# Attention and experts on one core: head outputs and score maxima re-laid by DMA, both score matmuls ahead of the maxima, the ends of six groups moved into the last two head pairs, and a ninth pair's maxima moved into the expert phase

## The reference

```python
x = L0_attn_z                                   # 4 batches x 1024 tokens x 128 features, float32
xn = _layernorm(x, axis=-1)
s = _L0_attn_ref(xn, ...)    # layernorm again, 16 heads of 8, softmax(q k^T / sqrt(8)) v, projection, + residual
g = _silu(_L0_ffn_ref(xn, ...))   # 8 experts 128 -> 512 -> 128 with exact gelu, top-2 softmax weights
x = x + s * g
```

## Time and profile before

| | before |
|---|---|
| median of 3 runs | 1122.94 us (1122.94 to 1123.12) |
| profiled execution: time, span | 1122.82 us, 1121.0 us |
| PE, DVE, ACT, POOL busy | 94%, 80%, 78%, 32% of the span |
| granted TensorE clock | 0.992 of full speed |

### The profile page before, as it was taken

The page is one execution under the profiler, slowest core; times in us unless marked ns, Lnnn a source line. Parts: engine busy times, 40 slices in busy tenths (PEclk is TensorE's granted clock), DMA queues, the critical chain, the costliest instruction groups (busy, mean ns, idle before and its releaser), DMA issues.

```text
span 1121.0 us, 17375 instructions
## 1 busy us (share of the span) xinstructions
PE 1054.6 (94%) x6009; PEld 449.6 (40%) x6041; DVE 893.9 (80%) x1647; ACT 870.7 (78%) x1189; POOL 361.1 (32%) x551
## 2 busy tenths in 40 slices
PE   4998999999999999999999999999999999999995
PEld 3666666666666666662212122212221221212123
DVE  5747778777878787657999999999999999999615
ACT  6876667676767676667888888888889888888981
POOL 4785657566666666452100010000000000000001
PEclk9999999999999999999999999999999999999999
DMA  5332221323141413223111111111111111111102
GB/s 180 119 106 59 82 72 50 95 50 104 31 119 37 113 35 93 50 68 106 45 45 30 45 44 46 31 44 34 55 40 35 44 44 45 30 44 30 31 1 76
DMA packets 84993, 67.42 MB, mean 60 GB/s; under 512 B 9277, under 2 KB 71402, under 8 KB 84906
## 3 DMA queue, kind: packets, MB, share of 16 engines
q1 hardware_dynamic: 84906, 66.32, 21.5%
HBM read 51.08 MB, written 15.20 MB: 59 GB/s over the span
## 4 chain that ended last, share of the span: by engine, by line
PE 31%; ACT 19%; DVE 3%; issue 2%; POOL 0%; ACTq 0%; DVEq 0%; POOLq 0%
ACT p_ring L798 18%; PE psum L987 13%; PE psum L965 10%; PE psum L928 4%; PE psum L1000 2%; DVE neg_max_half L1243 1%; PE psum L1021 1%; ACT o_sb L789 1%; DVE x_out L1315 0%; DVE msa_t L1296 0%; PE psum L939 0%; DVE y L1302 0%; PE psum L1013 0%; DVE y L1308 0%; ACT neg_max_t L774 0%
## 5 line engine op out<-in xcount | busy, mean ns | idle before, releaser
L798 ACT ACTIVATE p_ring<-psum 128x1024 f32<-128x1024 f32 x512 | 500.8, 1023 | 65.3 <-PE psum L965 61.6
L1243 DVE TENSOR_REDUCE neg_max_half<-psum 128x1 f32<-128x512 f32 x768 | 486.6, 685 | 37.3 <-PE psum L928 28.2
L965 PE MATMUL psum<-q_stack,k_stack 51*128 51x512 bf16 x1024 | 278.4, 382 | 13.3 <-ACT p_ring L798 4.1
L987 PE MATMUL psum<-p_ring,v_sb 128*9 128x512 f32 x2048 | 268.2, 596 | 0.4 <-ACT o_sb L789 0.4
L928 PE MATMUL psum<-k_max_stack,q_max_stack 48*128 48x512 bf16 x768 | 249.9, 384 | 5.8 <-DVE neg_max_half L1243 5.5
L761 ACT ACTIVATE h_hi<-psum,cols 128x512 fp32r<-128x512 f32 x192 | 132.5, 690 | 134.1 <-PE psum L878 133.2
L1261 DVE TENSOR_REDUCE neg_max_half<-psum 128x1 f32<-128x512 f32 x256 | 169.5, 684 | 55.1 <-PE psum L914 48.7
L634 POOL TENSOR_TENSOR h_lo<-h_split,h_hi 128x512 fp32r<-128x512 f32 x128 | 164.8, 1292 | 134.0 <-ACT h_split L764 133.8
L965 PEld LDWEIGHTS psum<-q_stack,k_stack 51*128 51x128 bf16 x1024 | 60.1, 94 | 305.8 <-ACT p_ring L798 281.8
L584 POOL CAST neg_max_parts<-neg_max_rest 128x16 bf16<-128x16 f32 x32 | 6.3, 198 | 509.6 <-DVE neg_max_rest L1252 509.5
L876 PE MATMUL psum<-xn_t_hi,w_hi 128*128 128x512 f32 x256 | 144.6, 565 | 0.7 <-DVE neg_max_half L1261 0.5
(11 more groups left out here) (123 smaller groups left out, 1023.8 us busy)
## 6 DMA issues: line engine op xcount, KB each, us to landing
expert_w_bc<-expert_w_dram SPq DMA_DIRECT2D x64, 256.0 KB, 4.9
k_rows_dram<-qk_parts SPq DMA_DIRECT2D x24, 256.0 KB, 3.1
q_max_stack<-q_rows_dram SPq DMA_DIRECT2D x64, 96.0 KB, 2.5
k_max_stack<-k_rows_dram SPq DMA_DIRECT2D x64, 96.0 KB, 2.5
q_stack<-q_rows_dram SPq DMA_DIRECT2D x64, 96.0 KB, 2.5
k_stack<-k_rows_dram SPq DMA_DIRECT2D x64, 96.0 KB, 2.5
q_rows_dram<-qk_parts SPq DMA_DIRECT2D x8, 384.0 KB, 2.6
xz<-in_L_attn_z_dram SPq DMA_DIRECT2D x8, 256.0 KB, 3.5
```

The source lines that it names most:

```text
L798: act.activation(p_sb[:, n % PR, a, :, :].rearrange("p h t -> p (h t)"), scores_bank[s % 2], ACT.Exp, scale=SCALE).then_inc(S("P"), 1)
L965: i = pe.matmul(scores_bank[s % 2][:, hh * TG:(hh + 1) * TG], k_s[rows, slot, kt * P:(kt + 1) * P], q_s[rows, slot, a * TG:(a + 1) * TG], ...
L987: i = pe.matmul(o_bank[at:at + VR, :], v_sb[:, b * KT + kt, 2 * (p % PB) + hh, :], p_sb[:, n % PR, a, hh, :], start=(kt == 0), stop=(kt == ...
L1243: dve.tensor_reduce(mx[:, p % MXR, c, hh * NT + t:hh * NT + t + 1], ring_bank(("max", u)), AX.X, ALU.max, negate=True).then_inc(S("R"), 1)
```

## The change

- **Maxima.** `m_t` and `neg_max_t` are gone. `sp_store_max` now stores `nmp` straight from its 128 partitions, transposing by its access pattern: 128 x 48 bf16 elements, each its own run of 2 bytes in DRAM. `neg_parts(p)` waits for the store of pair p-2.
- **Heads' outputs.** `o_t` and `head_out` are gone for pairs 0 to 30. At block 2 of the next pair `sp_heads` sends the output rows of `o_sb` to their place in `heads` (4 DMAs of 8 rows of 2 KB) and the sums to `den` spread over 128 partitions (4 DMAs of 32 runs of 64 bytes); at block 5 DVE takes reciprocals of [128 x 16] (`head_rden`), SP stores them to DRAM (block 6) and loads them back broadcast to 8 partitions each (block 7, 4 DMAs). POOL multiplies whole groups (`normalise_heads`). `o_copy` now waits for those DMAs of two pairs before. Only the last pair is turned on PE (`last_out`, `last_turn`) and projected separately (`project_last`).
- **Scores first.** Inside `scores` both score matmuls come first and signal ACT, and then come the tiles of maxima; the first half of a block takes 2 of them, the second the rest.
- **Ends.** `project`, `sum_y`, `gate_y`, `y_turn` and `finish` of groups 0 to 5 run from block 243 on, one group in two blocks. The gate is formed in the expert phase with tanh for groups 0 to 6 (silu(x) = 0.5 x (1 + tanh(x/2)), the 0.5 in `finish`), and for group 7 as before at the end. All gating products are on DVE.
- **Nine pairs.** EARLY_PAIRS is 9; the early tiles come every 3/4 slot instead of every 27/32, and end at the same slot. 736 tiles are left for the 240 blocks.

```diff
-        EARLY_PAIRS = 8
+        EARLY_PAIRS = 9
...
-        EARLY_AT = [HT + 4 + (27 * m) // 32 for m in range(EARLY)]
+        EARLY_AT = [HT + 4 + (3 * m) // 4 for m in range(EARLY)]
...
+            upto = [min(len(SINGLES), -(-((n + a) * len(SINGLES)) // MAX_BLOCKS)) for a in range(2)]
+            return (upto[0], min(upto[0] + 2, upto[1]), upto[1])[half]
...
-        TAIL = BLOCKS - KT + O_TURN + 1
+        ENDS_FROM = BLOCKS - 2 * KT + 3
...
         def sp_store_max(sp, p):
-            sp.wait_ge(S("mTc"), p + 1)
-            sp.dma_start(m_dram[p], nmT[:, p % 2, :]).then_inc(S(f"m_st{p % 2}"), 16)
+            sp.wait_ge(S("nmp"), p + 1)
+            sp.dma_start(m_dram[p].rearrange("m c -> c m"), nmp[:, p % 2, :, :, :].rearrange("p h i t -> p (h i t)"),
+                         allow_slow_non_contiguous=True).then_inc(S(f"m_st{p % 2}"), 16)
...
+        def sp_heads(sp, p):
+            b, slot = p // PB, p % 2
+            sp.wait_ge(S("oe"), p + 1)
+            for hh in range(2):
+                h = 2 * (p % PB) + hh
+                for a in range(2):
+                    at = VC * (2 * hh + a)
+                    sp.dma_start(heads[DH * h:DH * (h + 1), 2 * b + a, :], o_sb[at:at + DH, slot, :])\
+                        .then_inc(S(f"o_st{slot}"), 16)
+            n = TG // den.shape[2]
+            for t in range(4):
+                sp.dma_start(den[t * n:(t + 1) * n, slot, :],
+                             o_sb[VC * t + DH:VC * t + VR, slot, :].rearrange("a (n k) -> a n k", n=n))\
+                    .then_inc(S(f"den{slot}"), 16)
...
+                if p > 0 and kt == 2:
+                    sp_heads(sp, p - 1)
+                if p > 0 and kt == 6:
+                    sp_rden_out(sp, p - 1)
+                if p > 0 and kt == 7:
+                    sp_rden_in(sp, p - 1)
...
         def neg_parts(p):
                 if p > 1:
-                    pool.wait_ge(S("mT"), p - 1)
+                    pool.wait_ge(S(f"m_st{p % 2}"), 16 * (p // 2))
...
+            def normalise_heads(b):
...
+                for a in range(2):
+                    g = 2 * b + a
+                    pool.tensor_tensor(heads[rows, g, :], heads[rows, g, :], rden_t[rows, b % 2, a, :], ALU.mult)\
+                        .then_inc(S("hn"), 1)
...
+                if p in (18, 25, PAIRS - 1):
+                    normalise_heads((18, 25, PAIRS - 1).index(p))
+            normalise_heads(B - 1)
...
+                def gate():
+                    wait(act, "acc", g, E - 1, E - 1)
+                    act.wait_ge(S("qp"), 2 * (g + 2))
+                    act.activation(gt, ffn[:, g, :], ACT.Tanh, scale=0.5).then_inc(S("gate"), 1)
...
             def o_copy(p):
                 if p > 1:
-                    act.wait_ge(S("ot"), p - 1)
+                    act.wait_ge(S(f"o_st{p % 2}"), 64 * (p // 2))
+                    act.wait_ge(S(f"den{p % 2}"), 64 * (p // 2))
...
-                for k, hh in enumerate((first, 1 - first)):
+                for hh in range(2):
                     rows = slice(HALF * hh, HALF * hh + SROWS)
                     i = pe.matmul(scores_bank[s % 2][:, hh * TG:(hh + 1) * TG], k_s[rows, slot, kt * P:(kt + 1) * P],
                                   q_s[rows, slot, a * TG:(a + 1) * TG], start=True, stop=True)
-                    if k:
-                        i.then_inc(S("S"), 1)
-                    for u in units[k::2]:
-                        max_scores(u)
+                i.then_inc(S("S"), 1)
+                for _, u in singles:
+                    max_scores(u)
...
+            def project_last(g):
+                pe.wait_ge(S("tmc_a" if g == BESIDE else "tmc"), 1)
+                pe.matmul(project_bank(g)[:, :], wp_last[:, :], msaT[:, g - BESIDE, :], start=False, stop=True)\
                     .then_inc(S("tp"), 1)
...
+                ends.setdefault(4 * g, []).append(lambda g=g: project(g))
+                ends.setdefault(4 * g + 2, []).append(lambda g=g: y_turn(g))
...
+                def gated():
+                    wait(dve, "gate", g, 1, 1)
+                    dve.scalar_tensor_tensor(ffn[:, g, :], gt, 1.0, ffn[:, g, :], ALU.add, ALU.mult)\
+                        .then_inc(S("gated"), 1)
...
+            def head_rden(p):
+                slot = p % 2
+                dve.wait_ge(S(f"den{slot}"), 64 * (p // 2 + 1))
+                if p > 1:
+                    dve.wait_ge(S(f"r_st{slot}"), 16 * (p // 2))
+                dve.reciprocal(rden[:, slot, :], den[:, slot, :]).then_inc(S("rd"), 1)
...
+                if p > 0 and kt == 5:
+                    head_rden(p - 1)
```

More of the change, by code:

```diff
@@ L766, in gelu @@
                     return step
[L767 to L774, removed]
+                def gate():
+                    wait(act, "acc", g, E - 1, E - 1)
+                    act.wait_ge(S("qp"), 2 * (g + 2))
+                    act.activation(gt, ffn[:, g, :], ACT.Tanh, scale=0.5).then_inc(S("gate"), 1)
+                plan = {i: [gelu(i)] for i in range(HT)}
+                if g < NG - 1:
+                    plan[4 * E + 6] = [gate]
+                return plan
             def hi(ns):
@@ L779, in _ @@
             prepare_first(pre, experts, {9: hi(range(2)), 12: hi(range(2, 4)), 18: hi(range(4, RAW))})
[L780 to L781 removed]
+            expert_phase(experts, pre, first={2 * (n - RAW) + 5: hi([n]) for n in range(RAW, 2 * E)})
             def o_copy(p):
@@ L804, in _ @@
             o_copy(PAIRS - 1)
-            for g in range(NG):
-                act.activation(ffn[:, g, :], ffn[:, g, :], ACT.Silu).then_inc(S("gate"), 1)
+            act.activation(ffn[:, NG - 1, :], ffn[:, NG - 1, :], ACT.Silu).then_inc(S("silu"), 1)
+            act.wait_ge(S("tm"), 1)
+            act.activation(msaT[:, 0, :], bank[0][0:2 * DH, :], ACT.Copy).then_inc(S("tmc_a"), 1)
         @block.tensor
@@ L990, in pv, with last_out, last_turn @@
                 i.then_inc(S("PV"), 1)
[L992 to L998, removed]
+            def last_out():
+                pe.wait_ge(S("oe"), PAIRS)
                 for j in range(TT):
-                    i = pe.transpose(to[:, j * P:(j + 1) * P], o_sb[:, p % 2, j * P:(j + 1) * P], ident[:, :])
+                    i = pe.transpose(o_bank[:, j * P:(j + 1) * P], o_sb[:, (PAIRS - 1) % 2, j * P:(j + 1) * P],
+                                     ident[:, :])
                 i.then_inc(S("ot"), 1)
[L1004 to L1013, removed]
+            def last_turn(a):
+                pe.wait_ge(S("od"), 1)
+                pe.wait_ge(S("P"), 2 * BLOCKS)
+                for j in range(TT):
+                    m = pe.transpose(bank[a][0:2 * DH, j * P:(j + 1) * P], msa[:, a, j, :], ident[:, :])
                 m.then_inc(S("tm"), 1)
@@ L1046, in _ @@
                 p, kt = divmod(n, KT)
-                halves, turns = block_items(n)
-                at = 2 * (n - TAIL)
+                halves = block_items(n)
+                at = 2 * (n - ENDS_FROM)
                 scores(2 * n, halves[0])
-                for kind, k in turns:
-                    m_t(k) if kind == "mT" else o_t(k)
                 for step in ends.get(at, []):
@@ L1062, in _ @@
             pv(BLOCKS - 1)
-            for at in range(2 * (BLOCKS - TAIL), 2 * BESIDE + 2):
+            for at in range(2 * (BLOCKS - ENDS_FROM), 4 * BESIDE + 1):
                 for step in ends.get(at, []):
                     step()
-            o_t(PAIRS - 1)
-            for step in (msa_turn, project, y_turn):
-                for g in range(0 if step is y_turn else BESIDE, NG):
+            last_out()
+            for g in range(BESIDE, NG):
+                project(g)
+            for a in range(2):
+                last_turn(a)
+            for step in (project_last, y_turn):
+                for g in range(BESIDE, NG):
                     step(g)
```

196 lines of the change are left out of this document (91 added, 105 removed).

## The result

| | before | after |
|---|---|---|
| median | 1122.94 us (4 runs) | 1580.35 us (4 runs, 1569.96 to 1580.8) |
| ratio to before | | 1.407, 95% interval 1.4005 to 1.4128 |
| span of the profiled run | 1121.0 us | 1568.2 us |
| first exp, last copy of outputs | 510.3, 1092.3 us | 586.3, 1555.3 us |
| granted TensorE clock | 0.992 | 0.84 |

The forecast was 1089 us, 1066 to 1124. The kernel is 41% slower, on the side of the first rival (chance 0.15, priced at 1151 for a store of 15 us).

What follows compares the result with a forecast made beforehand. PE was taken to bound the expert phase, and late second scores with closely coupled PE, ACT and DVE the attention. 1121.0 - 42 + 9 + 5 - 16 + 10 = 1087.0 us of span, plus 1.8: 1089 us, range 1066 to 1124.

Steps and rivals of the forecast that it cites:

- first rival: At head_rden, block 5: the store of 2-byte runs holds up DVE and the kernel gets slower, 1151 us; chance 0.15.
- part 5: SP's DMAs: an 8 us store of maxima delays the sums only if issued shortly before them, +10 us.
- 1, 30 pairs with maxima: Attention: with both scores first, a pair takes 16.8 us; -42 us, bounds -63 and -15.
- 2, expert phase: Expert phase: 32 more tiles on PE and more DVE work; +9 us, bounds +6 and +15.
- 3, ends beside the last two pairs: Last two pairs: the ends of six groups make PE late; +5 us, bounds +2 and +9.
- 4, tail: After the last output copy: 12.7 us in place of 28.7; -16 us, bounds -17 and -13.
- my formula: At block 5: lateness of the sums from a store issued at t, taking S; +10 us in total at 8 us.

Runs made afterwards that it cites:

- flat_store: The changed kernel with its store of the maxima not transposed, 128 runs of 96 bytes in place of 6144 of 2, maxima scrambled: 1080.5 us, ratio 0.9625.
- pe_turn_mixed: The changed kernel with maxima turned on TensorE and stored as before, score matmuls again alternating with tiles of maxima: 1110.5 us, ratio 0.9898.
- dve_eight: dve_turn with eight pairs' maxima in the expert phase in place of nine: 1086.0 us, ratio 0.967.
- four_byte: The changed kernel with the store in 3072 runs of 4 bytes in place of 6144 of 2, maxima scrambled: 1310.4 us, ratio 1.1675.
- late_in: The changed kernel with the reciprocals read back one pair later in SyncE's order: 1478.4 us, ratio 1.317.
- pool_queue: The changed kernel with the stores of pairs 9 to 31 issued from GpSimd's queue: 1444.0 us, ratio 1.2865.
- dve_turn: The changed kernel with maxima transposed on VectorE in 32x32 blocks and stored as 128 runs of 128 bytes: 1083.0 us, ratio 0.965.

## Why the prediction was wrong

One step failed, part 5, the DMAs: in its price (8 us for a store that took 25.1 to land) and in its reach (a wait added only for stores shortly before the sums, where each store cost about 7 us in the expert phase and 18 in the attention). The other parts stand, read in flat_store, whose store takes 2 us.

| step | forecast | measured in flat_store against before |
|---|---|---|
| 1, 30 pairs with maxima | -42 | -42.9 (first exp to last reduction: 503.6 for 546.5) |
| 2, expert phase | +9 | +12.2 (first exp at 522.5 for 510.3) |
| 3, ends beside the last two pairs | +5 | +4.1 (last reduction to last copy: 39.6 for 35.5) |
| 4, tail | -16 | -16.2 (12.5 for 28.7) |
| 5, stalls on the store | +10 | 0 here; +490 of span in the changed kernel |

In all 1121.0 - 42.9 + 12.2 + 4.1 - 16.2 = 1078.2, the span of flat_store.

**Part 1** was right with its mechanism. In flat_store, windows and waits of mid-attention, against the earlier trace rows:

```profile
840.00:980.00 140.00, 137.94 (x1024) 28.86 (x1024) 131.39 (x222) 133.12 (x144) 7.44 (x26) 1.00 0.21 54
```

```profile
ACT p_ring L853 <- PE psum L999: 16.7, 39, 1.6
```

and ACT's timeline, where the exps stood four in a row before:

```profile
784.86 11.99 ACT L853 ACTIVATE p_ring<-psum 128x1024 f32<-128x1024 f32 x12 [0.23 <-PE psum L999]
```

ACT is busy 133 of 140 us where it was 125, and from 560 to 1010 us waits 39 times for scores, 16.7 us in all, where it was 103 times and 52.8 us (over 490 us). `pe_turn_mixed` shows the order's share in this, 13 us. In `dve_eight` 32 more tiles cost 18.3 us, 0.57 each: the tile isn't hidden behind TensorE and ScalarE, and its price is near VectorE's pitch of 0.634.

**Part 2** was mis-sized. The bound of +6 to +15 held in flat_store and in dve_eight (13.3), but 32 tiles cost about 0.4 us each and not 0.25. The price of a tile was misread: the prediction divided 82.8 us by 256 tiles, but the row of 82.8 us holds 224 matmuls, so a tile is 0.37 us (in flat_store 92.0 us for 256, 0.36). With 32 x 0.37 = 11.8 in place of 8 its own sum gives about +13. The waits for VectorE grew too, to 17.1 us in flat_store from 10.4; what they add was not tried.

**Part 5**, as the prediction put it: "nearest are the small ones and I take 21 ns: 8 us." A packet of 2 bytes took 46 ns on average and a store 25.1 us to land. My bounds of 3.8 to 30 us held it, but my value came from packets 128 times larger, as if size alone mattered, and the chance of the rival was set by nearness to those. The model itself was wrong too: it took a store to be over when its packets are. In four_byte they are started within 5.5 us and the landing takes some 15.

The Trainium skill ("VectorE: DVE Perf Modes", The three transpose paths) gave the right warning, but the estimate by its factor, 9.3 us, is too small against the 25.1 us measured. (At 9.3 us my formula adds 6 us, not the 5 that the prediction says.)

The reach failed more. "It delays the sums only if it is issued shortly before them" leaves out two things that the runs show. With S = 25 the lateness t + S + 3 - 11.5, summed over all 22 stores of the attention but pair 31's, is about 270 us and would put the kernel at 1349. It took 1580. The expert phase gives 64 of the 490 us of span, 7 us for each of its nine stores before the first exp: input rows come late there (DVE waits 67.8 us for `xz`, up to 20.7 at once). I had costed none. In the attention the loss is 426 us, 18.5 for each of 23 stores, and 9.4 in four_byte. The missing link is SP's order: a DMA behind the store is held at issue and lands with it, SP waits for its landing, and the next pair's rows and sums come after that. Counted pair by pair in the trace of the changed kernel, over the 22 waits of VectorE longer than 1 us, the sums are issued about 280 us late in all and land about 60 us late. late_in took 102 us off by undoing one wait of SP, pool_queue 125 in the attention by taking the store out of SP's queue.

Why neither removes more is not shown. In pool_queue the lateness is in the landing of the sums (10.4 us), so a store slows DMAs of another queue as well. That the engines are busy with its packets does not explain it alone: in four_byte the records are empty for two thirds of the time to landing, and the loss still is half of the whole. Only fewer runs took the loss away (four_byte in part, flat_store and dve_turn in full). No run here makes the sums independent of the store while the store stays, and none tells whether the time goes into the writes of 2 bytes to DRAM or into the reads in SBUF.

## What to carry to other kernels

Count the runs of a DMA, not its bytes: 12 KB in 6144 runs cost 25 us to land where 128 runs cost 2, and halving the runs took away a little more than half of the damage. Price it by its time to landing: the records of its packets can end long before. When a price must be extrapolated far from the nearest row, forecast with the upper bound too, and follow it through every queue in program order: a slow DMA holds not only what waits for it but whatever the issuing engine would send next. A transpose in blocks on VectorE (235 ns) turned the same idea from 41% slower to 3.5% faster.

## What the runs showed of the hardware that was not expected

A DMA issued behind the store of 6144 runs holds SP's own instruction for 13.3 us, behind 3072 runs for 1.57 (0.35 otherwise). It looks as if only so many runs could stand ahead; no run here tests that. DMAs on another queue are slowed as well: the sums' 2 KB land after 10.4 us instead of 1.7.

A landing can come long after the last packet: about 7 us in the changed kernel and 9.7 us in four_byte, with no packet in the records.

GpSimd issued the store of 6144 runs in 2.24 us, and it landed in 21.9 us; the nine that SP kept in that kernel landed in 23.7.

The granted clock fell with the stalls, to 0.84 on average. In the changed kernel's timeline, 1.6 us after a wait of 17 us, PE's eight PV matmuls at 1529.77 take 1.90 us, and the next eight, at 1533.46, take 1.05. The windows of the same stretches, with the granted clock third from the end (0.50, which is 1.2 GHz, and 1.00, which is 2.4 GHz):

```profile
1529.70:1531.60 1.90, 1.90 (x10) 0.13 (x9) 0.33 (x1) 1.02 (x1) 0.00 (x0) 0.50 0.10 17
1533.40:1534.50 1.10, 1.10 (x12) 0.18 (x10) 1.00 (x2) 0.93 (x1) 0.00 (x0) 1.00 0.00 0
```

The second stretch has twice the clock of the first, and eight such matmuls take 1.05 us there where they took 1.90.
